# Graph 1's edge rounds spread over eight steps, messages in four parts, eight buffers for the placing's one-hots

## The chip, the cores and the metric

One core of one Trainium2 chip runs the whole program in one launch. The metric is the device time of a launch in microseconds; smaller is better. TensorE is called PE here, VectorE DVE, ScalarE ACT, GpSimd POOL, and SyncE SP.

## What is computed

Two blocks, one after the other, each added to its input:

```
x = x + gnn(layernorm(x), src, dst)          # graph 1: 6250 nodes, 100000 edges, 8 heads of 32
x = x + ffn(layernorm(x), edge_index)        # graph 2: 131072 edges, 4 heads of 4, router + 4 experts

# gnn (an attention over edges), the part that matters here
h = (x @ W) as [N, 8, 32];  a_src, a_dst = sums of h * att over the 32
alpha = leaky_relu(a_src[src] + a_dst[dst], 0.2)
ex = exp(alpha - a peak of the destination)
out = segment_sum(h[src] * ex) / segment_sum(ex)      # over the edges with the same dst
out = layernorm(elu(out + bias + x)) * ln_scale + ln_bias
```

The second block does the same kind of attention on graph 2, whose edges come unsorted, takes the two best of four experts for each node, and adds their weighted outputs.

## The kernel before, in words

Nodes stand in 49 tiles of 128. Graph 1's edges are cut into 832 chunks of 128 edges, each chunk with destinations in one tile, and eight chunks (CG) make a round: 104 rounds (NG1). Each engine has its own program, written out in Python, and runs it strictly in order; the engines meet at semaphores. The order in each program is the order of the code, so what a waiting instruction has behind it waits too.

A round e of graph 1's edges goes through these operations:

- POOL (L712 to L726) gathers the rows of eight chunks from the table in DRAM, h and a_src of each source, 264 numbers an edge, into one of three buffers G1. Four gathers at a time wait until PE has summed what the buffer held three rounds before (`p_sum`).
- SP (L551 to L557) reads the destinations, spread over all partitions, into DR. DVE's `rows` (L1501) makes of them the one-hots ST1.
- PE transposes ST1 (L1249), and ACT copies the result to S1 (L876). PE looks the eight chunks' destination terms up with ST1 (L1270), after it has loaded eight registers with the tiles' places.
- DVE's `terms` (L1494) reduces the lookups, `score` (L1509) makes the leaky_relu in three small instructions, ACT takes the exponential (L872), and `messages` (L1522) multiplies all eight chunks' rows by it, in one instruction of 2048 numbers a partition (L1526).
- PE sums each chunk by destination (L1259), one matmul of 264 columns, into one of three banks, and DVE's `add` (L1481) adds it to the tile's row in big (L1492). PE's sum c waits for add c - 3.

An iteration i of the loop handles rows for round i, terms, score and messages for round i - 1, and the sums and adds of round i - 2; the adds lag two chunks (LAG). On DVE, terms, rows, score, the last two adds of the round before, and the whole message instruction stand at the start of the iteration, and then come eight steps k, of which six have an add.

Beside this, graph 2's edges are sorted on the same engines. `sort_order` gives the operations with costs, and `sort_at(8 * i + k)` those for step k of iteration i; every engine's loop calls it in each step, from step 0 to 792, which is iteration 99. Masks of the tiles come in iterations 0 to 4 (`cmask`) and 8 to 22 (`pmask`, `pick`), words and codes in 23 to 32. From iteration 33 to 64 and from 66 to 97 stands the placing: 1024 steps, each with `onehots` on DVE (L2137, a one-hot of 576 columns into one of NB = 4 buffers Bv, after PE has placed what it held, `p_pl`) and, two steps later in the order, `place` on PE (L1151, L1152: two matmuls, 512 and 64 columns). Two or three of them fall into a step k. Every fourth has a `hot`, a matmul of 512 columns (L1143) and ACT's relu of it (L797), which makes the left-hand sides Av of four places; every sixteenth a `turn` (L1136, L791).

When the last add is made (L1549), the middle part starts on DVE (L1555), then graph 2's edges with the experts beside them, and the output.

Of the kernel before, what the change touches and what calls it, by code (L numbers as in the profile page):

```python
# [11 lines left out]
CG = 8  # L12
# [24 lines left out]
def build(nc, x_d, src_d, dst_d, W_d, as_d, ad_d, bias_d, lns_d, lnb_d, Wg_d, gas_d, gad_d, bg_d, gam_d, bet_d,  # L37
          W1_d, b1_d, W2_d, b2_d, ei_d, out_d):
    f32, i32, u32, i16, u16, f16, b16 = (mybir.dt.float32, mybir.dt.int32, mybir.dt.uint32, mybir.dt.int16, mybir.dt.uint16,
                                          mybir.dt.float16, mybir.dt.bfloat16)  # L40
    ALU = mybir.AluOpType
    ACT = mybir.ActivationFunctionType
# [3 lines left out]
    with ctx:  # L46
# [37 lines left out]
        NG1 = NC1 // CG  # L84
# [12 lines left out]
        x_f = sb("x_sb", [128, T * D])  # L97
# [100 lines left out]
        half, sgn = small4[:, 0:64], small4[:, 64:128]  # L198


        NB = 4
        src2, dst2 = g2.idx[:, 0:1024].bitcast(i32), xtmp(0, i32)
        bF2 = x_f[:, 1024:1536].bitcast(f16)
        msk = [x_f[:, 1536 + 512 * n:2048 + 512 * n].bitcast(f16) for n in range(3)]
# [17 lines left out]
        own = x_f[:, 1088:1104]  # L222
        nI, fI, fJ, fX, fY = xtmp(4, i32), xtmp(1, i32), xtmp(2, i32), xtmp(4, f32), xtmp(5, f32)
        Av = [x_f[:, 256 * n:256 * n + 256].bitcast(f16) for n in range(4)]
        Bv = [x_f[:, 1024 + 288 * n:1312 + 288 * n].bitcast(b16) for n in range(NB)]
        dcd = [x_f[:, 2176 + HW * n:2176 + HW * n + HW] for n in range(6)]

        def turn_at(k):
# [146 lines left out]
        def sort_at(n):  # L375

            return sort_slots[n] if n < len(sort_slots) else []
# [466 lines left out]
        def scalar_program(a):  # L844
            a.wait_ge(s_c, 11)
            a.wait_ge(s_bF1, 2)
            for b in range(NV, T + 1):
                n = b - NV
# [17 lines left out]


            for i in range(NG1 + 1):
                if i >= 1:
                    e = i - 1  # L870
                    a.wait_ge(v_z, 4 * e + 4)
                    a.activation(G1[e % 3][:, :, 256:264], z1b[:, e % 2, :, :], ACT.Exp).then_inc(a_ex, 1)  # L872
                    a.wait_ge(p_tp, e + 1)
                    if e >= 2:
                        a.wait_ge(p_sum, CG * (e - 1))
                    a.copy(S1[:, e % 2, :, :].rearrange("p c n -> p (c n)"), pbank[0][:, :].bitcast(b16)).then_inc(a_w32, 1)  # L876
                for k in range(CG):
                    for op in sort_at(i * CG + k):
                        a_sort(a, op)

# [65 lines left out]
            for kind, q in out_a:  # L946
                n, j = pe_tiles[q]
# [272 lines left out]
        def tensor_program(pe):  # L1220
# [22 lines left out]
            for i in range(NG1 + 2):  # L1243
                if 1 <= i <= NG1:
                    pe.wait_ge(v_oT, i)
                    if i >= 2:
                        pe.wait_ge(a_w32, i - 1)
                    for k in range(CG):
                        t = pe.transpose(pbank[0][:, :].bitcast(b16)[:, k * 128:k * 128 + 128], ST1[:, (i - 1) % 2, k, :], ident16[:, :])  # L1249
                    t.then_inc(p_tp, 1)  # L1250
                for k in range(CG):
                    c = (i - 2) * CG + k
                    if c >= 0:
                        if k == 0:
                            pe.wait_ge(v_msg, i - 1)
                            pe.wait_ge(a_w32, i - 1)
                        if c >= 3:
                            pe.wait_ge(v_add, c - 2)
                        pe.matmul(sbank[c % 3][:, 0:g1.R], S1[:, i % 2, k, :], G1[(i - 2) % 3][:, k, :],  # L1259
                                  start=True, stop=True).then_inc(p_sum, 1)  # L1260
                    if k == 3 and i < NG1:
                        if i == 0:
                            pe.wait_ge(s_tab, 1)
                            pe.wait_ge(s_map1, 4)
                        pe.load(regs, g1.tm[0:1, K1 * 128 + i * CG:K1 * 128 + i * CG + CG])
                        pe.wait_ge(v_oT, i + 1)
                        if i >= 1:
                            pe.wait_ge(v_z, 4 * (i - 1) + 1)
                        for n in range(CG):
                            t = pe.matmul(pbank[1][:, n * 48:n * 48 + 48], ST1[:, i % 2, n, :],  # L1270
                                          tab31s[:, bass.ds(pe.snap(regs[n], min_val=0, max_val=T * 16), 16), :], start=True, stop=True)
                        t.then_inc(p_ad, 1)
                    for op in sort_at(i * CG + k):
                        p_sort(pe, op)
# [76 lines left out]
        def vector_program(v):  # L1351
            c = Tick(s_v)
# [141 lines left out]
            def terms(e):  # L1494
                v.wait_ge(p_ad, e + 1)
                if e:
                    v.wait_ge(v_z, 4 * e)
                v.tensor_reduce(adt[:, :, :], pbank[1][:, 0:CG * 48].rearrange("p (c w h) -> p c h w", w=3, h=16), X,
                                ALU.add).then_inc(v_z, 1)

            def rows(i):  # L1501
                s = i % 2
                v.wait_ge(l_dr[s], 16 * (i // 2 + 1))
                if i >= 2:
                    v.wait_ge(p_tp, i - 1)
                v.tensor_scalar(ST1[:, s, :, :].rearrange("p c n -> p (c n)"), DR[:, s, :], pidx[:, 0:1], None,
                                ALU.is_equal).then_inc(v_oT, 1)

            def score(e):  # L1509
                s = e % 2  # L1510
                ar, zt = z1c[:, s, :, :], z1b[:, s, :, :]
                v.wait_ge(l_g[e % 3], 16 * CG * (e // 3 + 1))
                v.wait_ge(v_z, 4 * e + 1)
                v.tensor_tensor(ar, G1[e % 3][:, :, 256:264], adt[:, :, 0:8], ALU.add).then_inc(v_z, 1)
                v.wait_ge(v_z, 4 * e + 2)
                v.scalar_tensor_tensor(ar, ar, 0.2, ar, ALU.mult, ALU.max).then_inc(v_z, 1)
                v.wait_ge(v_z, 4 * e + 3)
                if e >= 2:
                    v.wait_ge(a_ex, e - 1)
                v.tensor_tensor(zt, ar, adt[:, :, 8:16], ALU.subtract).then_inc(v_z, 1)  # L1520

            def messages(e):  # L1522
                s = e % 2
                hv = G1[e % 3][:, :, 0:256].rearrange("p c (h k) -> p c h k", k=32)
                v.wait_ge(a_ex, e + 1)
                v.tensor_tensor(hv, hv, G1[e % 3][:, :, 256:264].unsqueeze(3).broadcast_to([128, CG, 8, 32]), ALU.mult).then_inc(v_msg, 1)  # L1526

            v.wait_ge(s_tab, 1)
            v.wait_ge(s_ready, 1)
            v.wait_ge(s_map1, 4)  # L1530
            for i in range(NG1 + 2):
                if 1 <= i <= NG1:
                    terms(i - 1)
                if i < NG1:
                    rows(i)
                if 1 <= i <= NG1:
                    score(i - 1)
                for k in range(LAG):
                    if i >= 3:
                        add((i - 2) * CG - LAG + k)  # L1540
                if 1 <= i <= NG1:
                    messages(i - 1)
                for k in range(CG):
                    if i >= 2 and k >= LAG:
                        add((i - 2) * CG + k - LAG)
                    for op in sort_at(i * CG + k):
                        v_sort(v, c, op, tile_counts)
            for n in range(NC1 - LAG, NC1):
# [800 lines left out]
```

## Time and profile before

| | us |
|---|---|
| median of 3 runs | 3158.18 (3156.61 to 3159.11) |
| the profiled execution | 3152.2 |
| its span | 3150.4 |
| PE busy | 2300.8 (73%) |
| DVE busy | 2228.1 (71%) |
| POOL busy | 1892.1 (60%) |
| ACT busy | 890.5 (28%) |

Mean granted clock of PE over the span is 0.85 of full speed. Graph 1's edge loop lasts from about 147 to 1751 us. In the profile's rows, a line such as L1526 is a line of the kernel, `x70` counts instructions, and the time in brackets or behind the last bar is idle time of that engine just before the instruction, with what ended it.

### The profile page before, as it was taken

Reading aid. Unit: us, or ns where it says so; the run is one execution under the profiler, and the core shown is the slowest. Engines: PE = TensorE matmul, PEld = TensorE weight load, DVE = VectorE, ACT = ScalarE, POOL = GpSimd, SP = SyncE. Lnnn points to the kernel's source line nnn. Section 1 sums busy time; section 2 is a strip of 40 time slices with the busy share of each in tenths; the row PEclk is TensorE's granted clock in tenths of the full one; section 3 lists DMA queues with packets and bytes.
Section 4 is the critical chain, followed back from the end, with each engine's and each line's share of the span. In section 5 each row is a group of like instructions: output and inputs, shape, how many; then the busy total and the mean of one; then the engine's idle time right before and its main releaser. Section 6 shows DMA issues by size and latency. Waiting matters only on the chain. (4 is left out here: it accounts for less than half of the span.)

```text
span 3150.4 us, 41423 instructions
## 1 busy us (share of the span) xinstructions
PE 2300.8 (73%) x11082; PEld 1414.8 (45%) x11166; DVE 2228.1 (71%) x5853; ACT 890.5 (28%) x2255; POOL 1892.1 (60%) x1969
## 2 busy tenths in 40 slices
PE   2677775577777767777776666978788777878745
PEld 1434443344444444444444444545455544545424
DVE  7577888988787888787876775365566565656558
ACT  6500000022222212222220453333333333333313
POOL 0556666566665666566657125677777777777730
PEclk9878886689888988898987776998899888989877
DMA  4423333233333333333335001232222322222257
GB/s 149 135 76 101 91 95 93 77 93 86 86 86 81 89 87 86 82 86 87 87 84 174 8 6 35 68 70 57 72 67 69 74 64 54 69 60 64 65 164 275
DMA packets 168323, 271.99 MB, mean 86 GB/s; under 512 B 45430, under 2 KB 87988, under 8 KB 168084
## 3 DMA queue, kind: packets, MB, share of 16 engines
q0 software_dynamic: 67008, 127.12, 17.8%
q1 hardware_dynamic: 101076, 142.09, 14.0%
q8 instruction: 100, 1.64, 0.2%
q14 instruction: 139, 1.14, 0.1%
HBM read 228.24 MB, written 40.84 MB: 85 GB/s over the span
## 5 line engine op out<-in xcount | busy, mean ns | idle before, releaser
L724 POOL DMA_INDIRECT Gb<-table,idx x560 | 665.8, 1189 | 423.0 <-PE pb L1259 268.6
L2137 DVE TENSOR_SCALAR x_sb<-iota,x_sb 128x576 bf16<-128x576 f16 x1024 | 401.5, 430 | 165.9 <-PE pb L1152 161.4
L1166 PE MATMUL pb<-big,early 128*128 128x512 f32 (+1 forms) x832 | 449.7, 647 | 49.1 <-ACT Gb L807 38.4
L1259 PE MATMUL pb<-Gb,Sall 128*128 128x264 f32 x1120 | 429.9, 487 | 72.1 <-DVE big L1492 71.5
L1180 PE MATMUL pb<-early,Gb 128*128 128x256 f32 x1568 | 440.6, 429 | 44.6 <-ACT Gb L807 41.7
L1151 PE MATMUL pb<-x_sb 128*128 128x512 bf16 x940 | 359.1, 425 | 154.0 <-DVE x_sb L2137 154.0
L724 POOL DMA_INDIRECT early<-table,idx x272 | 324.4, 1193 | 205.2 <-PE pb L1259 140.1
L1492 DVE TENSOR_TENSOR big<-big,pb 128x264 f32 x832 | 352.3, 423 | 128.6 <-PE pb L1259 71.1
L1180 PEld LDWEIGHTS pb<-early,Gb 128*128 128x128 f32 x1568 | 317.4, 213 | 125.0 <-ACT Gb L807 45.3
L658 POOL DMA_INDIRECT dl<-table,idx x288 | 282.3, 980 | 107.0 <-issue 94.0
L797 ACT ACTIVATE x_sb<-pb 128x512 f16<-128x512 f32 x256 | 152.9, 597 | 621.4 <-PE pb L1143 621.4
L658 POOL DMA_INDIRECT early<-table,idx x272 | 267.4, 983 | 82.9 <-issue 82.9
L658 POOL DMA_INDIRECT tab<-table,idx x272 | 265.0, 974 | 83.3 <-issue 82.0
L1259 PEld LDWEIGHTS pb<-Gb,Sall 128*128 128x128 f32 x1120 | 225.4, 230 | 156.2 <-DVE big L1492 95.6
L2204 DVE TENSOR_TENSOR idx<-pb,b2B 128x256 f32<-128x256 f32 x196 | 83.1, 424 | 298.4 <-PE pb L1180 298.3
L1259 PE MATMUL pb<-early,Sall 128*128 128x264 f32 x544 | 213.6, 499 | 39.8 <-DVE big L1492 39.6
L2276 DVE TENSOR_TENSOR acc<-acc,asall 128x20 f32 x832 | 149.7, 180 | 117.2 <-issue 21.2
L807 ACT ACTIVATE Gb<-pb,b1c 128x512 f32<-128x512 f32 (+1 forms) x208 | 137.1, 662 | 310.3 <-PE pb L1166 309.6
L1151 PEld LDWEIGHTS pb<-x_sb 128*128 128x128 f16 x1024 | 108.3, 106 | 256.3 <-DVE x_sb L2137 192.5
L1152 PE MATMUL pb<-x_sb 128*128 128x64 bf16 x1024 | 210.0, 205 | 9.4 <-DVE x_sb L2137 2.9
L1166 PEld LDWEIGHTS pb<-big,early 128*128 128x128 f32 x832 | 135.2, 203 | 103.3 <-issue 48.0
L1270 PE MATMUL pb<-early,STb 128*128 x832 | 116.0, 202 | 81.4 <-issue 79.4
(418 smaller groups left out, 3708.3 us busy)
## 6 DMA issues: line engine op xcount, KB each, us to landing
Sall<-dlT SPq DMA_DIRECT2D x208, 256.0 KB, 3.5
Y<-idx SPq DMA_DIRECT2D x96, 256.0 KB
big<-Y SPq DMA_DIRECT2D x16, 1024.0 KB, 10.9
x_sb<-in_x_dram SPq DMA_DIRECT2D x8, 1536.0 KB, 13.4
Gb<-table,idx POOLq DMA_INDIRECT x560
early<-table,idx POOLq DMA_INDIRECT x544
out_dram<-x_sb SPq DMA_DIRECT2D x24, 256.0 KB
dl<-table,idx POOLq DMA_INDIRECT x288
```

The source lines that it names most:

```text
L658: g.indirect_dma_start(out=Gt2[s][:, k, :], out_offset=None, in_=g2.table, in_offset=bass.IndirectOffsetOnAxis(ap=g2.idx[:, c:c + 1], axis ...
L724: g.indirect_dma_start(out=G1[i % 3][:, k, :], out_offset=None, in_=g1.table, in_offset=bass.IndirectOffsetOnAxis(ap=g1.idx[:, c:c + 1], a ...
L797: a.activation(Av[g % 4], hot_bank(g)[:, :], ACT.Relu).then_inc(a_av, 1)
L807: a.activation(hh[:, bi % 2, f, 0:nt * 128], pbank[b][:, 0:nt * 128], ACT.Gelu, bias=b1c[:, ei, f:f + 1]).then_inc(a_gel, 1)
L1151: pe.matmul(pbank[5 + 2 * w][:, :], A, Bv[n][:, 0:512], start=j % HB == 0, stop=j % HB == HB - 1)
L1152: pe.matmul(pbank[6][:, 64 * w:64 * w + 64], A, Bv[n][:, 512:HW], start=j % HB == 0, stop=j % HB == HB - 1).then_inc(p_pl, 1)
L1166: t = pe.matmul(pbank[b][:, 0:nt * 128], W1s[:, w, k, f * 128:f * 128 + 128], xT[:, t0:t0 + nt, k * 128:k * 128 + 128], start=k == 0, stop ...
L1180: t = pe.matmul(pbank[b][:, 0:D], hh[:, bi % 2, f, j * 128:j * 128 + 128], W2s[:, w, f, :], start=f == 0, stop=f == 3)
L1259: pe.matmul(sbank[c % 3][:, 0:g1.R], S1[:, i % 2, k, :], G1[(i - 2) % 3][:, k, :], start=True, stop=True).then_inc(p_sum, 1)
L1492: v.tensor_tensor(o, o, sbank[n % 3][:, 0:g1.R], ALU.add).then_inc(v_add, 1)
L2137: v.tensor_scalar(Bv[j % NB], iota16[:, 0:HW], winF[:, j:j + 1], bE[:, j:j + 1], ALU.is_equal, ALU.mult).then_inc(v_bv, 1)
L2276: v.tensor_tensor(o, o, sums2[c // 8 % 2][:, c % 8, :], ALU.add).then_inc(m["v_ad"], 1)
```

## The change

DVE's iteration is spread: each of eight steps has one add; terms stands in step 0, rows in step 1, score in step 2, and the message instruction is cut into four of two chunks each, in steps 4 to 7. ACT copies the transposes first and takes the exponential in step 3. PE's sums wait for the part of the messages that they read, before every second chunk, and the lookups go from step 3 to step 4. The placing's one-hots have eight buffers, four of them in free space of x_sb.

```diff
--- before.py
+++ after.py
@@ -198,7 +198,7 @@
         half, sgn = small4[:, 0:64], small4[:, 64:128]
 
 
-        NB = 4
+        NB = 8
         src2, dst2 = g2.idx[:, 0:1024].bitcast(i32), xtmp(0, i32)
         bF2 = x_f[:, 1024:1536].bitcast(f16)
         msk = [x_f[:, 1536 + 512 * n:2048 + 512 * n].bitcast(f16) for n in range(3)]
@@ -222,7 +222,7 @@
         own = x_f[:, 1088:1104]
         nI, fI, fJ, fX, fY = xtmp(4, i32), xtmp(1, i32), xtmp(2, i32), xtmp(4, f32), xtmp(5, f32)
         Av = [x_f[:, 256 * n:256 * n + 256].bitcast(f16) for n in range(4)]
-        Bv = [x_f[:, 1024 + 288 * n:1312 + 288 * n].bitcast(b16) for n in range(NB)]
+        Bv = [x_f[:, o + 288 * n:o + 288 * n + 288].bitcast(b16) for o in (1024, 10880) for n in range(4)]
         dcd = [x_f[:, 2176 + HW * n:2176 + HW * n + HW] for n in range(6)]
 
         def turn_at(k):
@@ -866,15 +866,16 @@
 
 
             for i in range(NG1 + 1):
+                e = i - 1
                 if i >= 1:
-                    e = i - 1
-                    a.wait_ge(v_z, 4 * e + 4)
-                    a.activation(G1[e % 3][:, :, 256:264], z1b[:, e % 2, :, :], ACT.Exp).then_inc(a_ex, 1)
                     a.wait_ge(p_tp, e + 1)
                     if e >= 2:
                         a.wait_ge(p_sum, CG * (e - 1))
                     a.copy(S1[:, e % 2, :, :].rearrange("p c n -> p (c n)"), pbank[0][:, :].bitcast(b16)).then_inc(a_w32, 1)
                 for k in range(CG):
+                    if k == 3 and i >= 1:
+                        a.wait_ge(v_z, 4 * e + 4)
+                        a.activation(G1[e % 3][:, :, 256:264], z1b[:, e % 2, :, :], ACT.Exp).then_inc(a_ex, 1)
                     for op in sort_at(i * CG + k):
                         a_sort(a, op)
 
@@ -1251,14 +1252,15 @@
                 for k in range(CG):
                     c = (i - 2) * CG + k
                     if c >= 0:
+                        if k % 2 == 0:
+                            pe.wait_ge(v_msg, 4 * (i - 2) + k // 2 + 1)
                         if k == 0:
-                            pe.wait_ge(v_msg, i - 1)
                             pe.wait_ge(a_w32, i - 1)
                         if c >= 3:
                             pe.wait_ge(v_add, c - 2)
                         pe.matmul(sbank[c % 3][:, 0:g1.R], S1[:, i % 2, k, :], G1[(i - 2) % 3][:, k, :],
                                   start=True, stop=True).then_inc(p_sum, 1)
-                    if k == 3 and i < NG1:
+                    if k == 4 and i < NG1:
                         if i == 0:
                             pe.wait_ge(s_tab, 1)
                             pe.wait_ge(s_map1, 4)
@@ -1519,30 +1521,30 @@
                     v.wait_ge(a_ex, e - 1)
                 v.tensor_tensor(zt, ar, adt[:, :, 8:16], ALU.subtract).then_inc(v_z, 1)
 
-            def messages(e):
-                s = e % 2
-                hv = G1[e % 3][:, :, 0:256].rearrange("p c (h k) -> p c h k", k=32)
-                v.wait_ge(a_ex, e + 1)
-                v.tensor_tensor(hv, hv, G1[e % 3][:, :, 256:264].unsqueeze(3).broadcast_to([128, CG, 8, 32]), ALU.mult).then_inc(v_msg, 1)
+            def messages(e, h):
+
+                o = slice(2 * h, 2 * h + 2)
+                hv = G1[e % 3][:, o, 0:256].rearrange("p c (h k) -> p c h k", k=32)
+                if h == 0:
+                    v.wait_ge(a_ex, e + 1)
+                v.tensor_tensor(hv, hv, G1[e % 3][:, o, 256:264].unsqueeze(3).broadcast_to([128, 2, 8, 32]), ALU.mult).then_inc(v_msg, 1)
 
             v.wait_ge(s_tab, 1)
             v.wait_ge(s_ready, 1)
             v.wait_ge(s_map1, 4)
             for i in range(NG1 + 2):
-                if 1 <= i <= NG1:
-                    terms(i - 1)
-                if i < NG1:
-                    rows(i)
-                if 1 <= i <= NG1:
-                    score(i - 1)
-                for k in range(LAG):
-                    if i >= 3:
-                        add((i - 2) * CG - LAG + k)
-                if 1 <= i <= NG1:
-                    messages(i - 1)
                 for k in range(CG):
-                    if i >= 2 and k >= LAG:
+                    if (i - 2) * CG + k >= LAG:
                         add((i - 2) * CG + k - LAG)
+                    if 1 <= i <= NG1:
+                        if k == 0:
+                            terms(i - 1)
+                        if k == 2:
+                            score(i - 1)
+                        if k >= 4:
+                            messages(i - 1, k - 4)
+                    if k == 1 and i < NG1:
+                        rows(i)
                     for op in sort_at(i * CG + k):
                         v_sort(v, c, op, tile_counts)
             for n in range(NC1 - LAG, NC1):
```

## Rows read from the trace of the kernel before

**Rows 1.** Busy us of PE, PEld, DVE, ACT, POOL by stretch; granted clock; DMA.

```profile
147.00:222.00 75.00, 52.04 (x230) 28.04 (x230) 55.05 (x128) 15.10 (x18) 39.89 (x34) 0.74 0.31 83
...
260.00:478.00 218.00, 160.70 (x687) 92.64 (x685) 181.38 (x361) 17.56 (x30) 139.85 (x125) 0.82 0.34 96
478.00:631.00 153.00, 89.29 (x310) 57.05 (x311) 131.19 (x199) 12.28 (x21) 95.45 (x76) 0.64 0.31 85
631.00:1122.00 491.00, 385.10 (x2138) 225.21 (x2178) 392.40 (x947) 119.32 (x223) 300.11 (x252) 0.88 0.33 87
...
1155.00:1643.00 488.00, 381.07 (x2136) 222.62 (x2177) 391.75 (x945) 117.50 (x219) 299.90 (x250) 0.90 0.33 87
```

**Rows 2.** Timeline, DVE, one placing round: start us, us, instruction, idle before.

```profile
1011.02 0.55 DVE L1498 TENSOR_REDUCE adt<-pb 128x128 f32<-128x384 f32 x1
...
1012.57 0.43 DVE L1492 TENSOR_TENSOR big<-big,pb 128x264 f32 x1
...
1013.56 2.28 DVE L1526 TENSOR_TENSOR early<-early 128x2048 f32<-128x2048 f32 x1
1015.76 1.78 DVE L2137 TENSOR_SCALAR x_sb<-iota,x_sb 128x576 bf16<-128x576 f16 x5
1018.99 0.43 DVE L1492 TENSOR_TENSOR big<-big,pb 128x264 f32 x1 [1.45 <-PE pb L1259]
...
1020.02 0.42 DVE L1492 TENSOR_TENSOR big<-big,pb 128x264 f32 x1
```

**Rows 3.** Costliest groups, 631 to 1122 us: busy us, mean ns, idle before.

```profile
L724 POOL DMA_INDIRECT Gb<-table,idx x172 | 205.9, 1197 | 128.5 <-PE pb L1259 88.5 <-issue 40.0
L2137 DVE TENSOR_SCALAR x_sb<-iota,x_sb 128x576 bf16<-128x576 f16 x510 | 200.0, 431 | 82.0 <-PE pb L1152 79.9
...
L1492 DVE TENSOR_TENSOR big<-big,pb 128x264 f32 x249 | 105.1, 422 | 14.6 <-DVE big L1492 6.7 <-PE pb L1259 5.2 <-issue 2.7
```

**Rows 4.** Timeline, PE, the same round, at the full clock.

```profile
1020.19 0.61 PE L1259 MATMUL pb<-Gb,Sall 128*128 128x264 f32 x2
...
1022.75 0.38 PE L1151 MATMUL pb<-x_sb 128*128 128x512 bf16 x1
...
1024.92 0.38 PE L1151 MATMUL pb<-x_sb 128*128 128x512 bf16 x1
...
1027.63 0.61 PE L1249 MATMUL pb<-ident,STb 128*128 128x128 bf16 x8
1028.08 0.66 PE L1259 MATMUL pb<-early,Sall 128*128 128x264 f32 x2
```

**Rows 5.** Timeline, all engines, about the same message instruction.

```profile
1005.59 1.23 PE L1259 MATMUL pb<-Gb,Sall 128*128 128x264 f32 x2
...
1007.58 1.23 PE L1259 MATMUL pb<-Gb,Sall 128*128 128x264 f32 x2
...
1012.65 0.26 ACT L872 ACTIVATE early<-zb 128x64 f32<-128x64 f32 x1 [0.48 <-DVE zb L1520]
...
1016.24 0.61 PE L1151 MATMUL pb<-x_sb 128*128 128x512 bf16 x1 [2.97 <-DVE x_sb L2137]
...
1017.36 0.60 ACT L797 ACTIVATE x_sb<-pb 128x512 f16<-128x512 f32 x1 [3.39 <-PE pb L1143]
```

**Rows 6.** As rows 1, three us behind that message instruction.

```profile
1015.50:1018.50 3.00, 2.26 (x7) 1.23 (x9) 2.04 (x6) 0.60 (x1) 2.21 (x2) 0.50 0.17 45
```

**Rows 7.** Costliest groups of DVE, 260 to 478 us.

```profile
L1492 DVE TENSOR_TENSOR big<-big,pb 128x264 f32 x120 | 50.7, 423 | 34.8 <-PE pb L1259 26.7 <-DVE big L1492 8.1
```

**Rows 8.** Timeline, POOL, the last gathers.

```profile
1726.77 3.05 POOL L724 DMA_INDIRECT Gb<-table,idx  x1 [0.30 <-issue]
1730.12 0.95 POOL L724 DMA_INDIRECT Gb<-table,idx  x1 [0.30 <-issue]
```

**Rows 9.** Timeline, DVE, the end of the edges.

```profile
1726.72 2.28 DVE L1526 TENSOR_TENSOR Gb<-Gb 128x2048 f32<-128x2048 f32 x1
...
1751.49 0.27 DVE L1555 MEMSET x_sb<- 128x256 f32 x1
```

## Prediction

> **What bounds the kernel now.** I began with the busy time by stretch [rows 1]. Graph 1's edge loop runs from about 147 to 1751 us, half of the span. Its last add is followed on DVE by the first instruction of the middle part at 1751.49 us [rows 9], and all that comes later hangs on that; so a microsecond saved in the loop is one saved at the end, unless a later start is set by something else. In the two placing stretches, 631 to 1122 and 1155 to 1643 us, DVE is busy for 392 of 491 us and 392 of 488, and PE for 385 and 381. Neither is full: DVE idles 98.6 and 96 us. The count of adds, 249 in the first [rows 3], gives 249 / 8 = 31.1 rounds, so a round takes 491 / 31.1 = 15.8 us, and DVE is busy in 12.6 of them.
>
> Then the timeline of one round [rows 2]. Terms, row one-hots and score stand together (1011.02 to 1012.57), then two adds, then one message instruction of 2.28 us, and only then the one-hots of the placing. PE used up its four one-hot buffers meanwhile: its next place, at 1016.24, comes after 2.97 us idle, put down to DVE's L2137 [rows 5]. The granted clock is then 0.50, the 1.2 GHz level, for three microseconds [rows 6]. In return DVE, which may be only four one-hots ahead, stops at once when PE is late or does its eight lookups: 1.45 us before 1018.99 [rows 2], and 79.9 of the 82.0 us idle before L2137 are put down to PE's place, L1152 [rows 3]. So the two engines wait for each other in turn; no engine is the bound. That is what must be weighed: how much of DVE's 3.2 us of waits a round goes.
>
> **The change part by part.** *DVE's own work.* From start to start: terms, rows and score take 1.55 us; one step of one add and two one-hots, 1018.99 to 1020.02, takes 1.03, eight of them 8.24; the message instruction holds DVE from 1013.56 to 1015.76, 2.20 [rows 2]. Together 11.99, and 12.1 with the odd 17th one-hot. No operation is added but for the split: four parts of 512 elements for one of 2048. No row has such a part. Between the 264 elements of the add, 422 ns [rows 3], and the 2048 of the message, 2284 ns [rows 2], an element costs 1.04 ns and an instruction about 148 ns. That makes 682 ns for a part. The next instruction starts 0.08 us before a message ends, so a part holds DVE for 0.60, and four for 2.40: 0.20 a round more, 21 us in the 104 rounds (832 adds). If nothing overlaps it is 4 x 0.682 - 2.20 = 0.53 a round, 55 us. A gain has no source, since the elements are the same. I take 0.20, as other work stands between the parts and the rows show it starting early. DVE's floor is 12.3 us a round.
>
> On this the Trainium skill speaks against the change. VectorE: DVE Perf Modes, in its section on the TRN2 errata, says that each SBUF-source instruction pays a fixed latency, and gives (N + 151) / 0.96 ns for an fp32 tensor_tensor. The duration agrees with the 2284 ns here, but the next instruction starts before its end. By the page alone the split would cost 4 x 691 - 2291 = 473 ns a round, 49 us in all, and the forecast would be 28 us later.
>
> *PE's own work.* No matmul is added. At the full clock two steps take 1022.75 to 1024.92, 2.17 us, so eight take 8.7; the transposes hold it for 0.45 (1027.63 to 1028.08); the lookups with the loading of their eight registers fill the gap from the sum at 1020.19, about 0.45 of its own, to the place at 1022.75, 2.1 us [rows 4]. With 0.3 for a turn and the odd place that is 11.5. Three waits on v_msg are added: the parts are made a round before PE wants them, so they cost nothing; were they late, PE would wait and with it DVE's add two steps on.
>
> *Coupling.* A one-hot now waits for the place eight back, three to four steps, not for the step before. The add, two behind the sum, becomes what holds DVE to PE. I followed a round with the numbers above. In steps 4 to 7 DVE needs 1.03 + 0.60 = 1.63 us each, and PE 2.1 more in step 4. DVE can do steps 4 and 5 behind the finished sums, 3.3 us, which is nearly all of PE's 1.1 + 2.1. In steps 5 to 7 PE, at 1.1 each, comes back to DVE. In steps 0 to 2 DVE has terms, rows or score beside 1.03, about 0.5 more each, and again PE is the faster. So the stall of 2.97 us before the places goes, and most of that behind the lookups; what comes last next is DVE itself. I leave 0.7 us of waits a round (of 3.2): step lengths vary, and PE has only 0.8 us to spare. A round takes 13.0 us. The saving is 2.75 x 62.2 rounds = 171 us. With no waits at all it is 12.3 a round, 44 us more.
>
> *The lookups* move one step later. They want rows of the next round, now DVE's step 1, and the terms, step 0: both are past when PE is in step 4. Terms wants them a half round later. Nothing on DVE waits.
>
> *ACT* no longer waits for the score at the round's start. The copy of the transposes goes first. In step 3 it waits for the score of step 2, and behind that wait stand the relu of hot (0.60 [rows 5]) and what PE places with it. The place that needs a relu comes three steps later, about 3.3 us, against a wait of below one step. The exponential, 0.26 us [rows 5], is wanted by the first part in step 4, one step of 1.03 us later. Cost taken: nothing; if this cover is gone, it is a rival below.
>
> *POOL.* A gather takes 1.2 us with 0.3 between [rows 3]. That is 8 x 1.5 = 12.0 us a round, close to the new 13.0. But the mean holds a freeze: the gather at 1726.77 begins with the message instruction of 1726.72 and takes 3.05 us, the one at 1730.12 takes 0.95 [rows 8, 9]. So without freezes it is 10.0 a round. Four blocks of 0.6 with other work between hold a gather for below 0.6 each, at worst 2.4, more likely less than today's 2.0 (12.0 - 10.0). The score stands two steps later, so a gather has more time. Cost taken: nothing; bounds -0 and +0.4 a round.
>
> *Elsewhere.* From 260 to 478 us DVE idles 36.6 us [rows 1] in 120 / 8 = 15 rounds, 34.8 of it before the adds (26.7 for PE, 8.1 for the add before) [rows 7]. Spread adds remove the second and I take half of the first; less 3 for the split: 18 us. From 478 to 631 DVE is busy for 131 of 153 [rows 1], with chains of its own: 5 us. From 147 to 222 it is busy for 55 of 75, partly filling: 5 us. In the last rounds POOL's gathers follow each other [rows 8] and set the pace: nothing.
>
> Sum: 171 + 18 + 5 + 5 = 199 us. The profiled execution took 3152.2 us: 2953. The median of the runs stands 6.0 above it: 2959.
>
> **The rivals.** *PE's clock stays as it is.* Granted 0.88 [rows 1] means 24% of the time at half rate, 3.8 us a round. At the low level a step takes 1005.59 to 1007.58, 1.99 us [rows 5], for 1.09. That costs 3.8 x (1 - 1.09 / 1.99) = 1.7 a round, and PE needs 13.2, over DVE's floor. With 1.2 of mutual waits, 14.4 a round: 1.35 x 62.2 = 84 saved, 14 elsewhere, 3060. For it: PE keeps a hole of its own in each round, while it loads registers, within the 2.1 us of the lookups. Against: the fall in rows 6 follows the 2.97 us that this change removes.
>
> *ACT's exponential takes the place of the waits removed.* If DVE runs two steps ahead of PE, the relu of step 2 ends late and the first part waits for relu and exponential: about 0.9 us, with the semaphores 1.0 a round. Over the 97 rounds that have sorting work: 3056. For it: a strict order on ACT. Against: after step 2 DVE has just done its longest steps, and PE is close behind.
>
> *The waits only move*: DVE stops at the add where it stopped at the one-hot, and the round stays at 15.8. 3158. The lead of three steps speaks against it.
>
> *Slower: the parts freeze POOL four times.* If each part held a gather for today's 2.0 us, not for its own length, POOL would need 10.0 + 8.0 = 18.0 a round, 2.2 over today's 15.8; over the 97 rounds that have sorting work this is 213 us, 3371. It decides when a part costs a gather more than (15.8 - 10.0) / 4 = 1.45 us. The freeze in rows 8 ends with the message instruction, which speaks against it.
>
> GPSIMD Engine Reference, Key points, says that DVE instructions with two SBUF inputs contend for GpSimd's SBUF interfaces; the trace agrees on the 3.05 us gather. It gives no price.
>
> **How the numbers follow.** My case, 2915 to 3010: 0.62. PE's clock, to 3065: 0.17. ACT: 0.10. The waits only move: 0.04. Slower by POOL or otherwise: 0.05. Elsewhere below 2915: 0.02. The range reaches from DVE's floor, 2959 - 44 = 2915, to 3065, past both middle rivals and past the split without overlap (+34). About 0.2% is what a measurement tells from no change. Faster 0.92, same 0.03, slower 0.05.
>
> **What would show it.** Right: rounds of about 13 us from 33 to 97; DVE busy above 90% there; the idle before L2137 down from 82 us to below 20 in a placing stretch; parts of 0.68 us; PE's granted clock above 0.93; no 3 us gathers. Wrong: DVE waits of a microsecond before each first part (ACT); low clock as before with DVE's waits put down to PE's sum (PE); the score waiting for gathers (POOL).

## The result and the profile after

The changed kernel takes 2931.9 us (median of 4 runs, 2929.3 to 2936.2) beside 3157.4 us of the kernel before (4 runs): a ratio of 0.930, 95% interval 0.929 to 0.932. The profiled execution took 2934.4 us, its span 2932.6 us, 217.8 us less than before.

The page of the changed kernel, part 1 and the clock in 40 slices:

```profile
PE 2249.9 (77%) x11082; PEld 1391.0 (47%) x11166; DVE 2210.3 (75%) x6165; ACT 896.2 (31%) x2255; POOL 1773.1 (60%) x1969
...
PEclk9988996589999889999887769988998989999868
```

PE and DVE are busy for 51 and 18 us less than before, so little of the gain is work; it is idle time. The busy time by stretch of the changed kernel (columns as in [rows 1]; the bounds are DVE's row one-hots of rounds 0, 8, 23, 33, 64, 66, 97, 99, and its last add):

```profile
147.40:251.90 104.50, 78.63 (x345) 44.03 (x346) 83.11 (x227) 18.28 (x23) 59.67 (x58) 0.79 0.35 97
251.90:446.00 194.10, 153.42 (x680) 83.10 (x677) 180.02 (x403) 20.04 (x31) 120.89 (x123) 0.90 0.39 105
446.00:600.80 154.80, 94.73 (x321) 57.50 (x321) 132.27 (x232) 12.58 (x22) 94.82 (x79) 0.60 0.32 86
600.80:1003.90 403.10, 359.82 (x2118) 217.20 (x2159) 383.86 (x1040) 119.36 (x222) 258.60 (x249) 0.92 0.40 105
1035.50:1435.60 400.10, 357.13 (x2125) 216.39 (x2166) 383.42 (x1038) 118.58 (x219) 254.19 (x249) 0.93 0.40 105
1467.80:1533.50 65.70, 46.93 (x199) 29.40 (x197) 44.11 (x109) 7.75 (x14) 34.60 (x35) 0.87 0.62 183
```

In the placing DVE is busy for 383.9 of 403.1 us and 383.4 of 400.1, 95 and 96%, for 80% in [rows 1]. The starts of DVE's row one-hots in the timelines of both kernels, and the end of its last add, give what each stretch lost:

| rounds | before, us | after, us | difference |
|---|---|---|---|
| 0 to 8 (first masks, offsets) | 112.1 | 104.5 | -7.6 |
| 8 to 23 (masks and picks) | 218.0 | 194.2 | -23.8 |
| 23 to 33 (words, codes) | 153.8 | 154.7 | +0.9 |
| 33 to 64 (placing) | 490.2 | 403.1 | -87.1 |
| 64 to 66 (decode) | 33.5 | 31.6 | -1.9 |
| 66 to 97 (placing) | 488.1 | 400.1 | -88.0 |
| 97 to 99 (decode) | 34.8 | 32.2 | -2.6 |
| 99 to the last add | 73.4 | 65.7 | -7.7 |

The sum is -217.8 us, the whole difference of the spans: nothing behind the loop gave anything back. A placing round takes 403.1 / 31 = 13.0 us, for 15.8.

Some of the costliest groups of the changed kernel in the first placing stretch, 600 to 1004 us:

```profile
L2139 DVE TENSOR_SCALAR x_sb<-iota,x_sb 128x576 bf16<-128x576 f16 x512 | 196.2, 424 | 0.0
L724 POOL DMA_INDIRECT Gb<-table,idx x169 | 175.0, 1035 | 103.9 <-PE pb L1261 60.6 <-issue 43.3
...
L1494 DVE TENSOR_TENSOR big<-big,pb 128x264 f32 x249 | 104.4, 419 | 16.9 <-PE pb L1261 10.1 <-issue 6.1
...
L1530 DVE TENSOR_TENSOR Gb<-Gb 128x512 f32<-128x512 f32 x80 | 54.4, 680 | 0.0
```

The idle before the one-hots (L2139; it was L2137 in the kernel before) is 0.0, where [rows 3] have 82.0 us. DVE's idle is now 19.2 us in 31 rounds, 0.6 a round, 16.9 of it before the adds. A piece of DVE's timeline of the changed kernel, from step 7 of one round on:

```profile
701.97 0.68 DVE L1530 TENSOR_TENSOR Gb<-Gb 128x512 f32<-128x512 f32 x1
702.57 0.76 DVE L2139 TENSOR_SCALAR x_sb<-iota,x_sb 128x576 bf16<-128x576 f16 x2
703.25 0.42 DVE L1494 TENSOR_TENSOR big<-big,pb 128x264 f32 x1
703.59 0.55 DVE L1500 TENSOR_REDUCE adt<-pb 128x128 f32<-128x384 f32 x1
704.06 0.76 DVE L2139 TENSOR_SCALAR x_sb<-iota,x_sb 128x576 bf16<-128x576 f16 x2
```

A part of 512 elements lasts 0.68 us, and what follows starts 0.60 us after it; nothing stands idle between. The low clock has not gone. In the same trace, the lookups of a round, with PE's idle before them (1.36 us put down to "issue": no engine held PE, and what its program has there is the loading of eight registers), and the granted clock, 0.57, in three microseconds from their end:

```profile
725.16 1.21 PE L1272 MATMUL pb<-early,STb 128*128 x8 [1.36 <-issue]
```

```profile
725.90:728.90 3.00, 3.00 (x12) 1.61 (x12) 2.21 (x6) 0.60 (x1) 1.96 (x2) 0.57 0.40 90
```

Read in slices of a quarter of a microsecond from 640 to 1000 us, the clock falls to the low level 16 times, and each fall comes 0.5 to 2.4 us behind the end of such an idle time of 0.9 to 1.7 us before the lookups. In the same 360 us of the kernel before it falls 19 times. Ten of these falls come within 1.6 us of the end of PE's wait for one-hots, as the one in [rows 6]; eight come over 5 us behind it, and 0.1 to 2.3 us behind the loads.

### The profile page after: what moved, and what is told of

It reads as the page before. It is cut to its first block and busy times, and to the rows that moved or that the text cites. A ratio compares the mean times of both kernels' runs of the same rounds, so it can differ in the third digit from the quotient of the medians.

```text
span 2932.6 us, 42047 instructions
## 1 busy us (share of the span) xinstructions
PE 2249.9 (77%) x11082; PEld 1391.0 (47%) x11166; DVE 2210.3 (75%) x6165; ACT 896.2 (31%) x2255; POOL 1773.1 (60%) x1969
## 5 line engine op out<-in xcount | busy, mean ns | idle before, releaser
L724 POOL DMA_INDIRECT Gb<-table,idx x560 | 584.4, 1044 | 361.0 <-PE pb L1261 199.2
L1261 PE MATMUL pb<-Gb,Sall 128*128 128x264 f32 x1120 | 413.7, 468 | 55.8 <-DVE big L1494 55.7
L2139 DVE TENSOR_SCALAR x_sb<-iota,x_sb 128x576 bf16<-128x576 f16 x1024 | 392.8, 425 | 0.0
L724 POOL DMA_INDIRECT early<-table,idx x272 | 285.1, 1048 | 169.1 <-PE pb L1261 100.2
L1152 PE MATMUL pb<-x_sb 128*128 128x512 bf16 x940 | 342.8, 410 | 1.1 <-DVE x_sb L2139 0.8
L658 POOL DMA_INDIRECT early<-table,idx x272 | 266.2, 979 | 82.9 <-issue 82.9
L2206 DVE TENSOR_TENSOR idx<-pb,b2B 128x256 f32<-128x256 f32 x196 | 83.1, 424 | 294.4 <-PE pb L1181 293.8
L1261 PEld LDWEIGHTS pb<-Gb,Sall 128*128 128x128 f32 x1120 | 211.0, 219 | 135.8 <-issue 57.6
L1261 PE MATMUL pb<-early,Sall 128*128 128x264 f32 x544 | 207.0, 483 | 33.5 <-DVE big L1494 33.3
L807 ACT ACTIVATE Gb<-pb,b1c 128x512 f32<-128x512 f32 (+1 forms) x208 | 137.0, 662 | 307.2 <-PE pb L1167 306.5
L874 ACT CAST Sall<-pb 128x1024 f32<-128x1024 bf16 x104 | 105.2, 1012 | 397.9 <-PE pb L1250 396.4
L1530 DVE TENSOR_TENSOR Gb<-Gb 128x512 f32<-128x512 f32 x280 | 190.8, 681 | 0.7 <-ACT Gb L878 0.7
```

The lines of the kernel that those rows point to most:

```text
L658: g.indirect_dma_start(out=Gt2[s][:, k, :], out_offset=None, in_=g2.table, in_offset=bass.IndirectOffsetOnAxis(ap=g2.idx[:, c:c + 1], axis ...
L724: g.indirect_dma_start(out=G1[i % 3][:, k, :], out_offset=None, in_=g1.table, in_offset=bass.IndirectOffsetOnAxis(ap=g1.idx[:, c:c + 1], a ...
L1152: pe.matmul(pbank[5 + 2 * w][:, :], A, Bv[n][:, 0:512], start=j % HB == 0, stop=j % HB == HB - 1)
L1530: v.tensor_tensor(hv, hv, G1[e % 3][:, o, 256:264].unsqueeze(3).broadcast_to([128, 2, 8, 32]), ALU.mult).then_inc(v_msg, 1)
L2139: v.tensor_scalar(Bv[j % NB], iota16[:, 0:HW], winF[:, j:j + 1], bE[:, j:j + 1], ALU.is_equal, ALU.mult).then_inc(v_bv, 1)
```

## The experiments

All are timed beside the kernel before, in three sets. In set 1 the kernel before takes 3151 us, in sets 2 and 3 it takes 3713 and 3717: there ACT and DVE often start an instruction late, and the profile puts that down to "remote" (another core or an unknown queue) or to "issue". What made these two sets slower isn't known. The chips of the three sets bear the numbers 7, 8 and 7, so the chip alone doesn't explain it. Times are compared within a set only. The changed kernel was timed in sets 2 and 3 but not in set 1, whose kernels are compared with it by their ratios to the kernel before (0.930 for the changed kernel) or, where said, by their times (2931.9 us). A line of the same code stands a line or two apart in different kernels (PE's place is L1151 before and L1152 after). "Round" is a placing round, from the row one-hots of rounds 33 and 64.

| run | set | us | ratio to before (95%) | round, us |
|---|---|---|---|---|
| eight buffers alone | 1 | 3027.1 | 0.961 (0.958 to 0.964) | 13.7 |
| all but the buffers | 1 | 3013.1 | 0.956 (0.954 to 0.959) | 14.1 |
| messages whole, in step 4 | 1 | 2920.3 | 0.926 (0.924 to 0.928) | 12.7 |
| exponential first on ACT | 1 | 2970.5 | 0.941 (0.938 to 0.944) | 13.7 |
| the changed kernel | 2 | 3555.8 | 0.957 (0.955 to 0.959) | 14.2 |
| four parts in one step | 2 | 3579.0 | 0.962 (0.960 to 0.965) | 14.3 |
| lookups in step 3 | 2 | 3539.2 | 0.953 (0.950 to 0.956) | 13.6 |
| lookups in halves | 2 | 3470.7 | 0.934 (0.931 to 0.936) | 13.0 |
| the changed kernel, again | 3 | 3554.0 | 0.956 (0.953 to 0.958) | 14.1 |
| lookups in halves, again | 3 | 3463.7 | 0.932 (0.930 to 0.934) | 12.8 |
| halves, messages whole | 3 | 3560.5 | 0.959 (0.956 to 0.962) | 14.1 |
| the same, adds three behind | 3 | 3619.8 | 0.973 (0.971 to 0.976) | 15.4 |

As a measure, 360 us of the placing, 640 to 1000 us, of the kernel before and of the changed kernel:

```profile
640.00:1000.00 360.00, 282.24 (x1565) 164.56 (x1595) 287.12 (x692) 87.00 (x163) 219.38 (x184) 0.88 0.33 87
```

```profile
640.00:1000.00 360.00, 321.21 (x1916) 194.68 (x1952) 344.46 (x934) 107.25 (x198) 234.30 (x224) 0.93 0.40 105
```

**Eight buffers alone.**

```diff
-        NB = 4
+        NB = 8
```

> The kernel before with eight one-hot buffers for the placing and nothing else. My theory (DVE and PE wait for each other in turn, and it takes both the longer lead and the spread order to end it): DVE may lead by the two steps that the add allows, but four and a half us of it without a one-hot remain at the head of a round, so of PE's 2.97 us idle about half stays; a placing round goes from 15.8 to about 14.6 us, 3157 - 1.2 x 62 = 3083 us. Rival A, the buffers carry all: about 2960. Rival B, only the order matters: 3157, and the idle before L2137 moves to the add.

It brings 124 us, where 74 were expected: between the theory and rival A. The same stretch, and what PE and DVE waited for in it, with PE's wait of the kernel before for comparison:

```profile
640.00:1000.00 360.00, 291.28 (x1852) 173.91 (x1850) 326.70 (x802) 102.82 (x190) 242.21 (x211) 0.99 0.38 100
```

```profile
PE pb L1151 <- DVE x_sb L2137: 55.0, 22, 3.0
```

```profile
PE pb L1151 <- DVE x_sb L2137: 42.0, 26, 2.1
PE pb L1270 <- issue: 25.8, 23, 1.5
```

```profile
DVE big L1492 <- PE pb L1259: 24.2, 28, 1.4
```

A line gives the wait in us, the number of times, and the longest. The first is of the kernel before, 2.5 us a time; the second and third are of this one. PE now waits for one-hots 42.0 us in 26 rounds, 1.6 a round, about the half of 2.97 that the theory had. What it had not is the clock, which went from 0.88 to 0.99. That the clock made the 50 us more than expected fits, and no run separates it. DVE's own wait has moved from the one-hots to the add, 24.2 us, as rival B had it, but it is smaller there (60.2 us before L2137 in the kernel before).

**All but the buffers.**

```diff
-        NB = 8
+        NB = 4
```

> The changed kernel with four one-hot buffers again, its order kept. My theory: DVE may lead PE by one step, so PE's step with the lookups (3.2 us) stalls it for about 1.2 us a round: 2932 + 1.2 x 62 = 3006 us, with the idle back in front of the one-hots. Rival A (the buffers carry all): about 3080 or more. Rival B (only the order matters): 2932.

3013 us for the 3006 of the theory, and neither rival. DVE's waits in the stretch:

```profile
DVE x_sb L2139 <- PE pb L1153: 24.4, 36, 1.9
DVE big L1494 <- PE pb L1261: 9.3, 10, 1.4
```

The wait before the one-hots is back, 24.4 us, put down to PE's place. The order alone brings 138 us, the buffers alone 124, and both together 219 against the 3151 us of this set, or 225 against the 3157 of the result: they overlap by some 40, and neither is enough alone.

**The messages whole, in step 4.**

```diff
-                        if k >= 4:
-                            messages(i - 1, k - 4)
+                        if k == 4:
+                            messages(i - 1, 0)      # one instruction of 2048 elements
```

> The changed kernel with the messages in one instruction of 2048 elements, in step 4; PE waits for it once a round. My theory: the 2.2 us stand beside PE's lookups in its step 4, which take it as long, so PE is not starved; and the three instructions less give DVE 0.2 us a round: 2932 - 21 = 2911 up to 2940. Rival, the split is what ended PE's idle: PE runs out of one-hots for 1 to 2 us a round as before, low clock with it, 2932 + 62 to 124 = 2994 to 3056. POOL's gathers get back their freeze of 2 us, mean near 1.19 us instead of 1.05.

2920 us, 12 us less than the changed kernel by the times and 14 by the ratios, whose intervals (0.924 to 0.928, 0.929 to 0.932) just stand apart. In the traces graph 1's loop is 14.7 us shorter. The stretch, PE's waits, and POOL's gathers in it:

```profile
640.00:1000.00 360.00, 323.43 (x1969) 195.25 (x1968) 346.10 (x864) 108.56 (x202) 267.15 (x228) 0.94 0.41 108
```

```profile
PE pb L1272 <- issue: 33.1, 29, 1.5
PE pb L1261 <- DVE big L1494: 2.8, 1, 2.8
```

```profile
L724 POOL DMA_INDIRECT Gb<-table,idx x153 | 178.3, 1165 | 61.8 <-issue 40.5 <-PE pb L1261 21.3
```

PE waits for no one-hot, though DVE is in one instruction for 2.28 us: it is in its lookups then (a message from 720.02 us, PE without a place from 720.29 to 722.62). So the split did not end PE's starving; the longer lead with the rest of the order did. Whether a message instruction in another step than the lookups would be covered as well, this run doesn't say. What the split costs is somewhat below the 21 us of the forecast. It does one thing more, for POOL: a gather takes 1.17 to 1.20 us with whole messages and 1.04 to 1.06 with parts.

**The exponential first on ACT.**

```diff
                 if i >= 1:
+                    a.wait_ge(v_z, 4 * e + 4)
+                    a.activation(G1[e % 3][:, :, 256:264], z1b[:, e % 2, :, :], ACT.Exp).then_inc(a_ex, 1)
                     a.wait_ge(p_tp, e + 1)
...
-                    if k == 3 and i >= 1:
-                        a.wait_ge(v_z, 4 * e + 4)
-                        a.activation(G1[e % 3][:, :, 256:264], z1b[:, e % 2, :, :], ACT.Exp).then_inc(a_ex, 1)
```

> The changed kernel with ACT's exponential ahead of its copy at the start of a round, as before; DVE's score stays in step 2. If ACT's place in the order matters: ACT stands until DVE's step 2, the relus of steps 0 and 1 stand behind it and PE's next hot behind them, 1 us a round or more in the placing: above 2994 us. If ACT has the slack that its 30 per cent of busy time suggests: 2932 within 6.

2970.5 us: neither number, 39 us over the changed kernel by the times, 35 by the ratios. In the timeline of this kernel, step 2 of a round:

```profile
708.53 0.23 DVE L1521 TENSOR_TENSOR zb<-zc,adt 128x64 f32<-128x64 f32 x1
...
708.79 0.26 ACT L872 ACTIVATE Gb<-zb 128x64 f32<-128x64 f32 x1 [3.69 <-DVE zb L1521]
...
708.95 0.99 ACT L876 CAST Sall<-pb 128x1024 f32<-128x1024 bf16 x1
...
709.84 0.60 ACT L797 ACTIVATE x_sb<-pb 128x512 f16<-128x512 f32 x1
...
710.50 0.39 PE L1143 MATMUL pb<-x_sb 128*128 128x512 f16 x1 [1.49 <-ACT x_sb L797]
```

DVE's score ends at 708.76. ACT has stood for it since the round began; then come the exponential, the copy, and only then the relu of a hot that PE had finished at 707.05. PE's next hot waits 1.49 us for that relu, and DVE's adds for the sums behind it:

```profile
DVE big L1493 <- PE pb L1260: 30.8, 36, 2.4
```

That is 30.8 us from 640 to 1000, for 8.5 in the changed kernel: a chain of three engines, through one that is busy for 28% of the time.

**The four parts in one step**, one after the other in step 4, in set 2.

```diff
-                        if k >= 4:
-                            messages(i - 1, k - 4)
+                        if k == 4:
+                            for h in range(4):
+                                messages(i - 1, h)
```

> The changed kernel with its four parts of the messages one after the other in step 4, so that the split stays and only its spreading goes. Theory: the message block beside PE's lookups starves nobody, and three more instructions cost 0.2 us a round against the kernel with one instruction (2920): 2941 us, at worst 0.5 a round, 2972. Rival, the split itself costs nothing and the spreading costs (by the later parts, or by the gathers): 2920. The gathers' mean is near 1.19 us, since the four parts follow each other without a gap.

The numbers expected for this and the next two are for the times of set 1. As differences, +9 was expected (at worst +40, by the rival -12) and +23 us measured (3579.0 for 3555.8). The gathers' mean stayed near 1.02 to 1.06, not 1.19, so even short instructions without a gap let most of them in. Why the time is not nearer to that of the whole message can't be told in this set, where PE is late for other reasons.

**The lookups in step 3.**

```diff
-                    if k == 4 and i < NG1:
+                    if k == 3 and i < NG1:
```

> The changed kernel with PE's lookups in step 3, as before. Theory: PE's 3.2 us stand one step earlier, where DVE has its short step 3 and still the parts of 4 and 5 ahead; the add of step 5 waits for the sum of step 3, which is made: 2932 to 2945 us. Rival, the place of the lookups carries a good share of the gain, since DVE's add comes to wait for the sum behind them: 0.5 us a round or more, 2963 and above.

3539 us for 3556, 17 us less where 0 to 13 more were expected, with intervals that overlap by a hair (0.950 to 0.956 and 0.955 to 0.959). The rival, 31 us or more on top, is out: that the change moved the lookups to step 4 brought nothing.

**The lookups in halves.** PE loads four registers and looks four chunks up in step 3, and the other four in step 5; only the second half tells DVE.

```diff
-                    if k == 4 and i < NG1:
+                    if k in (3, 5) and i < NG1:
...
+                        n0 = 0 if k == 3 else 4
+                        pe.load(regs[n0:n0 + 4], ...)
...
+                        for n in range(n0, n0 + 4):
```

> The changed kernel with PE's eight lookups and their register loads in two halves, in steps 3 and 5. No work is added. In the changed kernel the granted clock falls to the low level in most rounds, each time behind the 1.2 to 1.5 us in which PE loads eight registers. Theory: halved holes leave the clock high (above 0.97 from 600 to 1000 us, for 0.92), PE is never behind DVE, and a placing round falls from 13.0 to about 12.5: 2932 - 31 = 2901 us. Rival, the holes have nothing to do with it, or DVE is the bound whatever PE's clock: 2932 within 6.

> PE's eight lookups and register loads in two halves, in steps 3 and 5, once more. Theory (the hole of the loads pulls the granted clock down, and low clock is what PE has no room for): granted clock above 0.97 in the placing for 0.92, rounds of 12.5 us for 13.0, 35 us less than the changed kernel beside it: 2897 us. Rival, the gain seen before (85 us) belongs to that chip's stretches: within 6 us of the changed kernel.

85 and 90 us less than the changed kernel beside it, where 31 and 35 were expected. It repeats, but both times in a slower set, so the rival of the second expectation is not settled. The stretch, 640 to 1000 us, of the changed kernel in set 3, and of the halves there:

```profile
640.00:1000.00 360.00, 304.47 (x1743) 180.24 (x1778) 317.03 (x846) 97.85 (x183) 206.25 (x201) 0.90 0.36 95
```

```profile
640.00:1000.00 360.00, 326.03 (x1970) 184.49 (x2006) 351.70 (x954) 111.39 (x205) 244.18 (x228) 0.99 0.41 107
```

PE's idle before the lookups and DVE's before the adds, in the changed kernel and then with the halves:

```profile
PE pb L1272 <- issue: 34.1, 25, 1.6
...
DVE big L1494 <- PE pb L1261: 23.8, 31, 1.7
```

```profile
PE pb L1273 <- issue: 14.2, 32, 0.7
...
DVE big L1496 <- PE pb L1261: 2.2, 5, 1.0
```

The clock is 0.99 for 0.90, DVE is busy for 98%, and a round takes 12.8 us. From 640 to 1000 us the clock falls twice for 16 times, and neither fall comes at a hole of the loads. But the clock isn't all that changed. The holes are shorter in their sum too, 14.2 us for 34.1, and PE's waits for ACT's copies and relus went from 14.9 us to 2.7. These three can't be told apart here. Nor is a hole of eight loads enough to pull the clock down: with eight buffers alone the same loads stand in one hole, 25.8 us in 23, and the clock is 0.99. How much of the 90 us would come where the changed kernel takes 2932 us was not measured. What disturbs set 3 is seen in ACT's waits in the changed kernel:

```profile
ACT x_sb L797 <- remote: 33.5, 9, 8.1
...
ACT x_sb L797 <- issue: 10.3, 5, 5.1
```

In the trace of the changed kernel that took 2934 us there is no such row in this stretch.

**The changed kernel again**, as the measure beside them.

> The changed kernel itself once more, as the measure for the three that run beside it: 2932 us within 6.

> The changed kernel again, as the measure for the three that run beside it. The kernel with PE's lookups in halves was timed beside it on a chip on which both kernels were slower (3556 us, with stretches in which no engine had work that the profile shows); this is to be repeated. 2932 us on a chip like the first.

3556 and 3554 us: in these sets 0.957 and 0.956 of the kernel before, for 0.930. The gain in microseconds is 157 and 163 for 225. Of the 622 us by which the profiled execution of set 3 is longer than that of the result, 518 lie behind graph 1's loop, where the change doesn't reach.

**Halves and whole messages together.**

```diff
-                        if k >= 4:
-                            messages(i - 1, k - 4)
+                        if k == 4:
+                            messages(i - 1, 0)      # on top of the lookups in halves
```

> Lookups in halves (steps 3 and 5) and the messages in one instruction in step 4. If the split costs its 0.2 us a round and nothing else, 15 to 21 us less than with the halves alone: 2880 us. If it was PE's 3.2 us of whole lookups that covered the message instruction, this cover is gone: PE stands for about a microsecond a round in step 5, its clock may fall again, and the time is not below that of the halves alone, up to 60 us above it.

```profile
640.00:1000.00 360.00, 294.62 (x1774) 175.23 (x1809) 317.29 (x788) 100.78 (x186) 241.67 (x207) 0.93 0.38 98
```

```profile
PE pb L1144 <- ACT x_sb L797: 14.5, 11, 4.3
...
PE pb L1152 <- DVE x_sb L2139: 8.4, 13, 1.2
```

97 us more than with the halves alone, over the 60 that the theory allowed, in the direction of the lost cover: the clock is down again, and PE waits for one-hots. But the longest of PE's waits are for ACT's relu, which is late in this set. So that whole messages want whole lookups beside them fits, and isn't shown.

**The adds three chunks behind**, on top of the last.

```diff
-            LAG = 2
+            LAG = 3
```

> As the one before, with the adds three chunks behind the sums and not two, so that DVE may lead PE by one step more and PE's sum needs the add of DVE's same step. If what is left of DVE's waits is the add on PE's sum (10 us in a placing stretch of the changed kernel): 10 to 20 us less than the one before. If DVE is the bound there: within 6 us.

```profile
PE pb L1261 <- DVE big L1496: 41.0, 25, 3.8
```

59 us more, where both theories had none. PE's sum takes one of three banks and waits for the add three before it. With the adds two behind, that add is DVE's in the step before; with three, it is in the same step, and PE now waits for DVE, 41.0 us from 640 to 1000. A longer lag for DVE was a shorter one for PE.

## Why the prediction was right

2959 us was forecast, 2931.9 measured; the gain is 225 us for 199. The mechanism, a placing round set by DVE, and its size held. The part on PE's clock did not, and of the smaller terms some were too low and one too high.

- **The mutual wait was the loss, and what ended it is the longer lead with the spread order.** Held, by the two experiments that undo one each: each alone leaves some 80 to 100 us of the gain out. Which part of the order is the one that counts is known only in part: not the split, nor the step of the lookups; ACT's order counts. The rival in which the waits only move is out: they went from 3.2 us a round to 0.6 (0.7 forecast). One row was misread: the 1.45 us before 1018.99 in [rows 2] are a wait of the add for PE's sum, and not for a free one-hot buffer.
- **A placing round of 13.0 us.** Held in both of its terms: DVE is busy for 12.4 us of it (12.3 forecast). The two stretches have 13.0 and 12.9, and give 175 us for 171.
- **The split at 0.20 us a round.** Held in its parts (0.68 us, 0.60 from start to start), and near in its sum of 21 us. The 12 to 14 us by the whole messages are what is left after the faster gathers gave something back (in the last stretch 65.7 us with parts, 68.5 with whole messages). The 49 us worked out from the Trainium skill, VectorE: DVE Perf Modes, the section on the TRN2 errata, are not borne out. As a duration its formula agrees (691 ns for a part, 680 measured), but the next instruction starts 0.08 us before the end.
- **PE's clock.** The reason given against the rival failed: the fall was tied to the 2.97 us without one-hots, and the low clock stays (0.92 and 0.93, forecast above 0.93) with that gone. It now comes behind PE's 0.9 to 1.7 us of register loads, which the rival had named. The trace of the kernel before had it already: 8 of its 19 falls in the 360 us came behind the loads, and [rows 6] is one of the others. The rival's price did not come: its 3.8 us of low clock a round became about 2, and PE is late for the adds by 10 us in a stretch only. That it cost so little wasn't forecast by a reason; the low clock was taken to be gone.
- **ACT at no cost.** The step holds for the change as made. That its place mattered was under-told: with the old order on ACT, 35 to 39 us of the gain go. The rival's 97 us were for waits at DVE's first part; the waits came at PE's hots and DVE's adds.
- **POOL at -0 to +0.4 us a round.** Mis-sized, and in the safe direction: gathers fell from 1.19 to 1.04 us, and the longest from 630 to 1000 us from 3.02 to 1.34. The slower rival is out.
- **"In the last rounds: nothing"** failed, by 7.7 us. POOL sets the pace there, and the gathers in that stretch, before and after, are:

```profile
L724 POOL DMA_INDIRECT Gb<-table,idx x29 | 34.4, 1186 | 9.2 <-issue 8.2 <-PE pb L1259 0.9
L724 POOL DMA_INDIRECT early<-table,idx x8 | 9.0, 1126 | 2.4 <-issue 2.1 <-PE pb L1259 0.3
```

```profile
L724 POOL DMA_INDIRECT Gb<-table,idx x28 | 28.0, 1000 | 9.8 <-issue 7.6 <-PE pb L1261 2.2
L724 POOL DMA_INDIRECT early<-table,idx x8 | 7.6, 944 | 2.8 <-issue 2.1 <-PE pb L1261 0.7
```

  37 gathers in 43.4 us became 36 in 35.6: 0.18 us less each, 6.7 of the 7.7. The price of the freeze had been taken from the rows and was not carried to the stretch where POOL is the bound.
- **Masks and picks, 18 us:** 23.8. I took half of DVE's wait for the sums as staying; 10.4 us of 26.7 stayed. The first masks gave 7.6 for 5, the decodes 4.5 that had no term.
- **Words and codes, 5 us:** +0.9, the one term that was too high. The granted clock is 0.60 there. DVE's waits before the adds only moved: 18.1 us before (7.7 for the add before, 5.2 for PE's sums, 5.2 "issue"), 18.4 after (16.5 for PE's sums, 1.9 for the add before). The split's 2 us come on top.

The rest of the difference is not the loop's: the profiled execution before lies 5.2 us under its median, the one after 2.5 over its own. The chances in the forecast add up to 0.91 for "faster", where 0.92 stands.

## What to carry to other kernels

Where two in-order engines feed each other, count in steps how far each may lead, through every buffer and every lagging operation, and set the lead to cover the other's longest block. Here that did more than cutting the block into parts: with the lead and the spread order an uncut instruction of 2.28 us starved nobody. It stood in the step of the other engine's longest block; whether it must, these runs leave open. An engine that is idle for two thirds of the time still needs its waits placed: what stands behind a wait is late for everyone. Look for the holes in TensorE's stream that are no wait at all, such as loads of registers, and spread them: of all the variants this gave the most on top of the change, though it was measured in the slower sets only.

## What the runs showed of the hardware that I had not expected

- The granted clock does not follow PE's busy share. With eight buffers alone PE is busy for 291 of 360 us and the clock is 0.99; in the changed kernel it is busy for 321 and the clock 0.93. In the latter each of 16 falls comes behind the hole of the loads, such as the 1.36 us before 725.16. In the former the holes of the loads, 1.1 us on the mean, bring none, and the holes before the one-hots, 1.6 us on the mean, bring three, each behind one of 2.0 to 2.1 us. What makes the difference between these holes isn't shown.
- A gather that starts inside a message instruction lasts as long as that still does and 0.82 us more (3.05 us at 1726.77 in [rows 8]). From 630 to 1000 us of the kernel before this holds for 24 of 190 gathers, which last 2.76 us on the mean and end 0.81 to 0.83 us behind the message; the others take 0.94 to 1.12. In the changed kernel 58 of 231 start inside a part of 0.68 us and last 1.19 on the mean, with the same 0.82. GPSIMD Engine Reference of the Trainium skill, Key points, names the shared interfaces; the price is these runs'.
- The same two programs took 3157 and 2932 us once and 3717 and 3554 another time, with nearly the same durations of single instructions on DVE and POOL (adds 421 and 425 ns, gathers 1044 and 1040 in the changed kernel), and with idle time on ACT and DVE that the profile puts down to "remote": 620 us before ACT's L807 and 560 before DVE's L2206, both behind graph 1's loop.
